# A two-layer graph attention kernel: node-id rows prepared one group ahead in the first layer, two transposes moved to the end of the step in the second

## The chip, the cores and the metric

The kernel runs on one core of a Trainium2 chip. A core has five engines with queues of their own that work in parallel and wait for each other through semaphores: PE (matmul), DVE (vector), ACT (activation), POOL (here it only issues gathers) and SP (plain transfers). The metric is the time of one execution on the device in microseconds (us); lower is better.

## The reference

The input is a graph of 3125 nodes with 128 features and 53125 edges, sorted by destination. Two attention layers run one after the other, each on the normalised node features and added to them.

```
h = relu(layernorm(x));  x = x + L0(h)     # e = leaky(a_src[src] + a_dst[dst]), 8 heads
h = relu(layernorm(x));  x = x + L1(h)     # e = q[dst] . k[src] / 4 + edge_attr @ We + be
# both: m = segment_max(e, dst); p = exp(e - m[dst]); out = segment_sum(p * v[src], dst) / segment_sum(p, dst)
```

L1 ends with an output projection and a layer norm. The edge attributes (32 per edge) are used by L1 alone, but their product with We is computed along with L0.

## The kernel before

Nodes are cut into 25 blocks of 125, edges into 416 tiles of 128. A tile and a block that meet are a "visit": 440 visits. 16 visits make a group (28 groups; the last has 8 visits), four visits a quarter. Each layer is one loop over `step(g)`, g from 0 to 29, written out in full, once for each engine. Its order on each engine is the order of the code; what ties the engines together are counting semaphores. In one step three groups are worked on:

- group g (`new`): its one-hot matrices S (edge x node in the block) are made by ACT (`one_hot`, L632 and L636, 4 visits at a time). The source rows are gathered from a table in memory into G by POOL (L528, one gather of 128 rows per visit, 16 per group). The destination side is spread to the edges by a matmul with ST, the transpose of S (`expand`, PE). DVE forms the scores.
- group g-1 (`mid`, called q): scores are transposed on PE (L874, L875; semaphore `scoreT`), scanned along the edges on DVE, and maxima are passed between visits by two small products on PE (`hop1`, L891, and `hop2`, L904). From the maxima follow differences DD (DVE), exponentials EP (ACT), their transposes on PE (L945, L946, `pT`), a factor per node (L951, `al_mm`, then ACT L682), and the softmax columns of PV (ACT L693, `pcols`).
- group g-2 (`old`, called r): DVE multiplies the gathered rows by the columns (`weigh`, L1408, four quarters), PE sums them by node (`sums`, L857, six batches of 3, 3, 2, 3, 3, 2 visits; `mm_done`), DVE adds the sums to `acc` (`add`, L1431, 16 of them).

How ST is made differs. In the second layer PE transposes S (`one_hot_T`, L828, four transposes per quarter) into one of two banks tp, and ACT copies it (`evac`, L642). In the first layer PE spreads a row of node ids over 125 partitions (`spread_ids`, L821, a matmul with ones, from `lid_ring`) into tp, and DVE compares it with the partition's own number (`node_rows`, L1220), which gives a bf16 ST_b. tp has two banks, so quarter 2 waits for the use of quarter 0. In the first layer tp[0] also takes the transposes of the edge attributes (L938, `a_T`), which ACT copies to attrT (L678, `a_Te`) for the product with We (L916).

POOL's order is plain: 16 gathers for each group, group after group, three groups deep. A function `pace` holds it back at every fourth gather by waits on PE's semaphores. In the first layer gather 0 of group g waits for `expanded` of the quarters 0 and 1 of group g-1 and for eight sums of step g-1, gather 8 for `scoreT` of step g, gather 12 for `hop1`. Those waits don't appear in the diff. In the second layer gather 8 waits for transposes and sums of the step before, and gather 0 waits for the first `weigh` of the group whose place in G it takes.

```python
                        wait(pool, s["expanded"], 4 * q + 2)
                        if r >= 0:
                            wait(pool, s["mm_done"], GV * r + 8)
```

## Time and profile before

| | us |
|---|---|
| median of 3 timed runs | 1561.53 |
| lowest, highest | 1558.28, 1563.58 |
| the profiled run | 1565.84 |
| its span, first to last instruction | 1564.1 |

In the profiled run PE is busy for 65% of the span, DVE for 60%, POOL for 56% and ACT for 41%. The first layer's loop takes roughly 60 to 730 us of the span, the second layer's 820 to 1520 us. Times in the rows further down count from the start of the span. The number in brackets at a row's end is how long the engine had stood idle before the instruction, and what ended it; "remote" and "issue" name no instruction. An operation's start on PE is its launch; its result can be seen later.

### The profile page before, as it was taken

Reading aid. Unit: us, or ns where it says so; the run is one execution under the profiler, and the core shown is the slowest. Engines: PE = TensorE matmul, PEld = TensorE weight load, DVE = VectorE, ACT = ScalarE, POOL = GpSimd, SP = SyncE. Lnnn points to the kernel's source line nnn. Section 1 sums busy time; section 2 is a strip of 40 time slices with the busy share of each in tenths; the row PEclk is TensorE's granted clock in tenths of the full one; section 3 lists DMA queues with packets and bytes.
Section 4 is the critical chain, followed back from the end, with each engine's and each line's share of the span. In section 5 each row is a group of like instructions: output and inputs, shape, how many; then the busy total and the mean of one; then the engine's idle time right before and its main releaser. Section 6 shows DMA issues by size and latency. Waiting matters only on the chain. (4 is left out here: it accounts for less than half of the span.)

```text
span 1564.1 us, 21265 instructions
## 1 busy us (share of the span) xinstructions
PE 1022.3 (65%) x4985; PEld 859.9 (55%) x4985; DVE 934.4 (60%) x3002; ACT 638.2 (41%) x1699; POOL 880.9 (56%) x926
## 2 busy tenths in 40 slices
PE   5546666656757766667475567666767767676775
PEld 4335554545545555555365456656656666565664
DVE  6446656556566655657823465656566565656577
ACT  5524343343434434422463344434344444444414
POOL 5756666666666666662056566665666555666400
PEclk9655556565565555655776687787776676778665
DMA  6322222222222222122133232322232222332201
GB/s 138 80 55 54 60 51 60 52 59 61 54 57 54 61 60 55 45 60 80 51 109 95 79 85 85 88 84 78 83 87 85 81 85 81 85 88 84 68 1 42
DMA packets 56924, 110.37 MB, mean 71 GB/s; under 512 B 17421, under 2 KB 31393, under 8 KB 56677
## 3 DMA queue, kind: packets, MB, share of 16 engines
q0 software_dynamic: 36288, 91.12, 22.5%
q1 hardware_dynamic: 19203, 17.39, 3.9%
q8 instruction: 47, 0.77, 0.2%
q10 hardware_dynamic: 1313, 0.50, 0.1%
q14 instruction: 73, 0.59, 0.1%
HBM read 100.60 MB, written 8.81 MB: 70 GB/s over the span
## 5 line engine op out<-in xcount | busy, mean ns | idle before, releaser
L528 POOL DMA_INDIRECT G<-table,idx_all x880 | 854.6, 971 | 524.2 <-issue 272.7
L857 PE MATMUL bank<-PV,S 128*125 128x144 f32 x1760 | 456.3, 420 | 134.2 <-DVE acc L1431 79.7
L857 PEld LDWEIGHTS bank<-PV,S 128*125 128x125 f32 x1760 | 379.8, 291 | 157.6 <-issue 82.5
L1431 DVE TENSOR_TENSOR acc<-acc,bank 125x144 f32 x880 | 260.3, 296 | 291.0 <-PE bank L857 155.4
L632 ACT ACTIVATE S<-iota_n,lid 128x125 f32<-128x125 f32 x880 | 275.8, 387 | 0.4 <-issue 0.4
L841 PE MATMUL bank<-qe,ST 125*128 x880 | 163.6, 355 | 93.4 <-DVE prod L1230 67.8
L841 PEld LDWEIGHTS bank<-qe,ST 125*128 125x128 f32 x880 | 152.6, 264 | 106.1 <-issue 106.1
L642 ACT ACTIVATE ST<-bank 125x512 f32<-125x512 f32 x110 | 63.7, 595 | 284.5 <-PE bank L828 153.2
L1408 DVE TENSOR_TENSOR PV<-G,PV 128x512 f32<-128x512 f32 x220 | 151.1, 688 | 22.4 <-issue 20.8
L636 ACT ACTIVATE S<-S,ones 128x500 f32<-128x500 f32 x220 | 156.6, 712 | 8.9 <-ACT S L632 1.9
L828 PE MATMUL bank<-ident,S 128*125 128x128 f32 x440 | 101.1, 369 | 30.7 <-issue 24.2
L828 PEld LDWEIGHTS bank<-ident,S 128*125 128x125 f32 x440 | 82.9, 263 | 38.5 <-issue 29.4
L1220 DVE TENSOR_SCALAR ST<-bank,vcol 125x512 bf16<-125x512 f32 x110 | 81.5, 743 | 33.2 <-remote 30.5
L1338 DVE TENSOR_TENSOR CCM<-bank,Vsel 128x32 f32<-128x32 f32 x56 | 10.7, 191 | 150.6 <-remote 116.0
L667 ACT ACTIVATE EP<-DD 128x256 f32<-128x256 f32 (+1 forms) x56 | 20.3, 363 | 189.5 <-DVE DD L1372 189.5
L1230 DVE TENSOR_TENSOR prod<-bank,G 128x512 f32<-128x512 f32 x110 | 74.6, 678 | 24.7 <-remote 19.8
L904 PE MATMUL bank<-D,HselT 8*128 8x16 f32 x224 | 51.9, 347 | 39.5 <-DVE D L1331 23.1
L904 PEld LDWEIGHTS bank<-D,HselT 8*128 8x128 f32 x224 | 46.4, 287 | 52.8 <-DVE D L1322 29.8
L1239 DVE TENSOR_REDUCE raw<-prod 128x32 f32<-128x512 f32 x110 | 74.3, 675 | 1.1
L682 ACT ACTIVATE AL<-bank 125x8 f32<-125x8 f32 x56 | 9.9, 177 | 156.3 <-PE bank L951 96.3
L875 PE MATMUL bank<-ident,sc 128*128 128x128 f32 x56 | 20.9, 373 | 69.6 <-issue 38.1
L916 PE MATMUL bank<-WeBD,attrT 128*128 128x32 f32 x208 | 49.0, 400 | 26.2 <-DVE CCM L1338 15.1
(219 smaller groups left out, 1125.7 us busy)
## 6 DMA issues: line engine op xcount, KB each, us to landing
G<-table,idx_all POOLq DMA_INDIRECT x880
prod<-in_edge_attr_dram SPq DMA_DIRECT2D x26, 224.0 KB
table<-G SPq DMA_DIRECT2D x12, 224.0 KB
bias_rows<-qe SPq DMA_DIRECT2D x1, 1664.0 KB
table<-h0b SPq DMA_DIRECT2D x8, 178.5 KB
out_dram<-G SPq DMA_DIRECT2D x8, 168.0 KB
prod<-in_edge_attr_dram SPq DMA_DIRECT2D x26, 30.0 KB
xs<-in_x_dram SPq DMA_DIRECT2D x1, 504.0 KB
```

The lines of the kernel that those rows point to most:

```text
L528: pool.indirect_dma_start(G[:, u, v, 0:w], None, table, bass.IndirectOffsetOnAxis(ap=idx_all[:, g * GV + v:g * GV + v + 1], axis=0)).then_ ...
L632: last = act.activation(S[:, u, v, :], iota_n[:, 0:BN], ACT.Abs, bias=lid[:, bass.ds(g * GV + v, 1)], scale=-1.0)
L636: act.activation(S[:, u, QV * j:QV * j + QV, :], S[:, u, QV * j:QV * j + QV, :], ACT.Relu, bias=ones[:, 0:1], scale=-1.0).then_inc(s.sem[" ...
L828: last = pe.transpose(tp[j % 2][0:BN, k * P:k * P + P], S[:, u, QV * j + k, :], ident[:, :])
L841: last = pe.matmul(ex[j % 2][:, k * F:k * F + F], ST[:, v, :], nodes[:, bass.ds(off, F)], start=True, stop=True)
L857: pe.matmul(sums_bank(p)[0:BN, at:at + H * SLOT], S[:, ur, v, :], PV[:, v, :, :].rearrange("p h k -> p (h k)"), start=True, stop=True).the ...
L904: last = pe.matmul(sm[:, 64 + GV * k:64 + GV * k + GV], HselT[:, :, :].rearrange("p v h -> p (v h)"), d[:, k, k:k + GV], start=True, stop= ...
L1220: ve.tensor_scalar(ST_b[:, QV * j:QV * j + QV, :], tp[j % 2][0:BN, :].rearrange("p (v e) -> p v e", v=QV), node, None, op0=ALU.is_equal).t ...
L1230: ve.tensor_tensor(prod[:, j % 2, :].rearrange("p (v f) -> p v f", v=QV), ex[j % 2][:, :].rearrange("p (v f) -> p v f", v=QV), G[:, u, QV ...
L1239: ve.tensor_reduce(raw[:, QV * j:QV * j + QV, :].rearrange("p v h -> p (v h)"), prod[:, j % 2, :].rearrange("p (c d) -> p c d", d=DH), AX. ...
L1408: ve.tensor_tensor(PV[:, QV * j:QV * j + QV, :, 0:DH], rows, PV[:, QV * j:QV * j + QV, :, DH:DH + 1].to_broadcast([P, QV, H, DH]), ALU.mul ...
L1431: ve.tensor_tensor(a, a, o, ALU.add).then_inc(s.sem["acc_added"], 1)
```

## The change

In the first layer all four id rows of group g+1 are spread and compared in step g, into the other half of ST_b, which now has two (`g % 2`). PE spreads quarters 0 and 1 after the third batch of sums and 2 and 3 before the fifth. DVE compares after its adds 7, 8, 11 and 13. The expansions 0 and 1 stand after the first and second batch of sums. The attribute transposes of group q are made in step q+1, right after the score transpose, and ACT copies them as its first operation of the step, ahead of esT; before, they were made in step q ahead of `pT`. In the second layer the transposes 0 and 1 of group g+1 are made at the end of step g on PE, and copied at the end of step g on ACT; the one-hots 2 and 3 come ahead of the copies 2 and 3, and PE's transposes 2 and 3 and expansions 0 and 1 change places.

```diff
-        ST_b = ST_[0:BN, :, :].rearrange("p v e -> p (v e)").bitcast(BF16)[:, 0:GV * P].rearrange("p (v e) -> p v e", v=GV)
+        ST_b = ST_[0:BN, :, :].rearrange("p v e -> p (v e)").bitcast(BF16).rearrange("p (d v e) -> p d v e", d=2, v=GV)
...
+                    if n == 0 and mid and q < AG:
+                        wait(act, a_T, q + 1)
+                        wait(act, a_mm, q)
+                        act.activation(attrT[:, :], tp[0][:, :], ACT.Copy).then_inc(a_Te, 1)
                     if mid and n == 0:
                         wait(act, s["scoreT"], q + 1)
                         wait(act, s["dd_ready"], 2 * q)
...
                         if g == 0:
                             one_hot(g, u, 0)
                             one_hot(g, u, 1)
-                        for j in range(new):
+                            evac(g, 0)
+                            evac(g, 1)
+                        for j in range(2, new):
+                            one_hot(g, u, j)
+                        for j in range(2, new):
                             evac(g, j)
-                            if j + 2 < new:
-                                one_hot(g, u, j + 2)
...
                         act.activation(eb_nat[:, bass.ds(q * (ATTR_C * H), ATTR_C * H)], sm[:, 256:256 + ATTR_C * H],
                                        ACT.Copy).then_inc(a_out, 1)
-                    if new:
-                        if n == 0 and has_attr(g, new):
-                            wait(act, a_T, g + 1)
-                            wait(act, a_mm, g)
-                            act.activation(attrT[:, :], tp[0][:, :], ACT.Copy).then_inc(a_Te, 1)
...
                         wait(act, s["mm_done"], GV * q)
                         act.activation(PV[:, :, :, DH:DH + k].rearrange("p v h k -> p (v h) k"),
                                        sT[:, 2 * P:(2 + k) * P].rearrange("p (k c) -> p c k", k=k), ACT.Copy).then_inc(s.sem["pcols"], 1)
+                    for j in range(min(quarters(g + 1), 2) if n else 0):
+                        evac(g + 1, j)
...
                     wait(pe, s["st_ready"], 4 * g + j - 1)
-                    if j == 0:
-                        wait(pe, a_Te, attr_done(g - 1))
+                    if j == 0 and g > 1:
+                        wait(pe, a_Te, attr_done(g - 2))
                     pe.matmul(tp[j % 2][0:BN, :], ones_b[32 * u:32 * u + 1, :], lid_ring[32 * u:32 * u + 1, j * QV * P:(j + 1) * QV * P],
                               start=True, stop=True).then_inc(s.sem["t_done"], 1)
...
-                        last = pe.matmul(ex[v // 8][:, v % 8 * width:(v % 8 + 1) * width], ST_b[:, v, :],
+                        last = pe.matmul(ex[v // 8][:, v % 8 * width:(v % 8 + 1) * width], ST_b[:, g % 2, v, :],
...
-                    if new and n == 0:
-                        spread_ids(g, u, i, 0)
-                        spread_ids(g, u, i, 1)
+                    ahead, ua, ia = quarters(g + 1), (g + 1) % UNROLL, (g + 1) // UNROLL
+                    if n == 0 and g == 0:
+                        for j in range(new):
+                            spread_ids(g, u, i, j)
...
                         pe.transpose(sT[:, 0:P], sc[:, :, :].rearrange("p v h -> p (v h)"), ident[:, :]).then_inc(s.sem["scoreT"], 1)
+                    if n == 0 and mid and q < AG:
+                        pe.wait_ge(s_attr[q % UNROLL], 48 * (q // UNROLL + 1))
+                        wait(pe, a_Te, q)
+                        wait(pe, s["st_ready"], 4 * g + 3)
+                        for k in range(QV):
+                            last = pe.transpose(tp[0][:, k * P:k * P + P], attr_in[:, q % UNROLL, k * P:k * P + P], ident[:, :])
+                        last.then_inc(a_T, 1)
                     if new:
                         pe.load(regs, offs[1 if n else 2][:, bass.ds(g * GV, GV)])
-                    if new and n:
+                    if n and g == 0:
                         one_hot_T(g, u, 0)
+                        one_hot_T(g, u, 1)
                     if 3 * old > 0:
                         sums(g, u, 0)
-                    for j in range(2, 0 if n else new):
-                        spread_ids(g, u, i, j)
+                    if new and n == 0:
+                        expand(g, 0)
                     if mid:
                         wait(pe, s["rh_ready"], q + 1)
                         wait(pe, s["x_done"], q)
@@ -892,8 +904,10 @@
                                   start=True, stop=True).then_inc(s.sem["hop1"], 1)
                     if 3 * old > 2:
                         sums(g, u, 1)
-                    if new and n:
-                        one_hot_T(g, u, 1)
+                    if new > 1 and n == 0:
+                        expand(g, 1)
+                    if new > 2 and n:
+                        one_hot_T(g, u, 2)
                     if mid:
                         wait(pe, s["x_done"], q + 1)
                         wait(pe, s["u_done"], q + 1)
@@ -904,11 +918,8 @@
                             last = pe.matmul(sm[:, 64 + GV * k:64 + GV * k + GV], HselT[:, :, :].rearrange("p v h -> p (v h)"),
                                              d[:, k, k:k + GV], start=True, stop=True)
                         last.then_inc(s.sem["hop2"], 1)
...
-                    if new and n == 0:
+                    if new and n:
                         expand(g, 0)
-                        expand(g, 1)
-                    if new > 2 and n:
-                        one_hot_T(g, u, 2)
                     if n == 0 and mid and q < AG:
                         wait(pe, a_Te, q + 1)
                         wait(pe, s["cc_mul"], q + 1)
@@ -918,25 +929,22 @@
                         last.then_inc(a_mm, 1)
                     if 3 * old > 4:
                         sums(g, u, 2)
-                    if new and n:
-                        expand(g, 0)
-                        expand(g, 1)
+                    for j in range(0 if n else min(ahead, 2)):
...
+                        spread_ids(g + 1, ua, ia, j)
                     if new > 3 and n:
                         one_hot_T(g, u, 3)
+                    if new and n:
+                        expand(g, 1)
                     if 3 * old > 6:
                         sums(g, u, 3)
                     if new > 2:
                         expand(g, 2)
                     if new > 3:
                         expand(g, 3)
+                    for j in range(2, 0 if n else ahead):
+                        spread_ids(g + 1, ua, ia, j)
                     if 3 * old > 8:
                         sums(g, u, 4)
-                    if n == 0 and has_attr(g, new):
-                        pe.wait_ge(s_attr[u], 48 * (i + 1))
-                        wait(pe, a_Te, g)
-                        for k in range(QV):
-                            last = pe.transpose(tp[0][:, k * P:k * P + P], attr_in[:, u, k * P:k * P + P], ident[:, :])
-                        last.then_inc(a_T, 1)
...
                     if 3 * old > 10:
                         sums(g, u, 5)
+                    for j in range(min(quarters(g + 1), 2) if n else 0):
+                        one_hot_T(g + 1, (g + 1) % UNROLL, j)
                 run_groups(step)
...
-                    def node_rows(j):
-                        if j >= new or n == 1:
-                            return
-                        wait(ve, s["t_done"], 4 * g + j + 1)
-                        wait(ve, s["expanded"], 4 * (g - 1) + j + 1)
-                        ve.tensor_scalar(ST_b[:, QV * j:QV * j + QV, :],
+                    def node_rows(to, j):
+                        if j >= quarters(to) or n == 1:
+                            return
+                        wait(ve, s["t_done"], 4 * to + j + 1)
+                        wait(ve, s["expanded"], 4 * (to - 2) + j + 1)
+                        ve.tensor_scalar(ST_b[:, to % 2, QV * j:QV * j + QV, :],
                                          tp[j % 2][0:BN, :].rearrange("p (v e) -> p v e", v=QV), node, None,
                                          op0=ALU.is_equal).then_inc(s.sem["st_ready"], 1)
...
-                    node_rows(0)
+                    if g == 0:
+                        for j in range(4):
+                            node_rows(g, j)
                     load_offsets(0)
                     weigh(0)
-                    node_rows(1)
                     load_offsets(1)
                     loop_max()
                     weigh(1)
                     edge_scans()
                     rescale()
                     edge_maxima()
-                    node_rows(2)
                     add(0)
                     visit_scans()
                     add(1)
                     carry()
-                    node_rows(3)
                     add(2)
                     weigh(2)
...
                     differences()
                     weigh(3)
                     add(7)
+                    node_rows(g + 1, 0)
                     shrink()
                     qk_product(0)
                     add(8)
+                    node_rows(g + 1, 1)
                     shrink_heads()
                     qk_sum(0)
                     add(9)
@@ -1474,10 +1485,12 @@
                     loop_weights()
                     qk_sum(1)
                     add(11)
+                    node_rows(g + 1, 2)
                     qk_product(2)
                     add(12)
                     qk_sum(2)
                     add(13)
+                    node_rows(g + 1, 3)
                     qk_product(3)
                     part_sum(1)
                     score_sum()
```

PE in the first layer, around the score transpose (L874, L875) between two steps. First before, then in the changed kernel, where these lines are L878 and L879; L951 is L959, L857 is L860, and L938 is L885.

```order
790 L951 MATMUL bank<-R,OHF 125x8
791 L857 MATMUL bank<-PV,S 125x144 x2
792 L821 MATMUL bank<-lid_ring,ones_b 125x512 x2
793 L874 MATMUL bank<-ident,es 128x128
794 L875 MATMUL bank<-ident,sc 128x128
795 L877 TENSOR_LOAD rows
796 L857 MATMUL bank<-PV,S 125x144 x3
797 L821 MATMUL bank<-lid_ring,ones_b 125x512 x2
798 L891 MATMUL bank<-RH,Hsel 8x32
```

```order
354 L959 MATMUL bank<-R,OHF 125x8
355 L860 MATMUL bank<-PV,S 125x144 x2
356 L878 MATMUL bank<-ident,es 128x128
357 L879 MATMUL bank<-ident,sc 128x128
358 L885 MATMUL bank<-ident,prod 128x128 x4
359 L888 TENSOR_LOAD rows
360 L860 MATMUL bank<-PV,S 125x144 x3
```

The two spreads L821 ahead of the score transpose are gone, and the four attribute transposes follow it.

DVE in the first layer, after the multiply of quarter 3 (L1408, now L1418). L1220, now L1230, is the compare, L1431, now L1441, an add.

```order
846 L1408 TENSOR_TENSOR PV<-G,PV 128x32x16
847 L1431 ISA
848 L1431 TENSOR_TENSOR acc<-acc,bank 125x144
849 L1383 TENSOR_SCALAR DF<-DF 8x1
850 L1431 ISA
851 L1431 TENSOR_TENSOR acc<-acc,bank 125x144
852 L1390 TENSOR_SCALAR R<-ident,DF 8x8
```

```order
844 L1418 TENSOR_TENSOR PV<-G,PV 128x32x16
845 L1441 ISA
846 L1441 TENSOR_TENSOR acc<-acc,bank 125x144
847 L1230 TENSOR_SCALAR ST<-bank,vcol 125x512
848 L1393 TENSOR_SCALAR DF<-DF 8x1
849 L1441 ISA
850 L1441 TENSOR_TENSOR acc<-acc,bank 125x144
851 L1230 TENSOR_SCALAR ST<-bank,vcol 125x512
852 L1400 TENSOR_SCALAR R<-ident,DF 8x8
```

Two of the four compares now stand after the adds 7 and 8, ahead of the scores of the same step. Before they came after the scores (L1278):

```order
867 L1278 SCALAR_TENSOR_TENSOR sc<-raw 128x128
868 L1431 ISA
869 L1431 TENSOR_TENSOR acc<-acc,bank 125x144
870 L1431 ISA
871 L1431 TENSOR_TENSOR acc<-acc,bank 125x144
872 L1260 TENSOR_TENSOR xs<-xs,rowv 125x128
873 L1220 TENSOR_SCALAR ST<-bank,vcol 125x512
874 L1211 TENSOR_LOAD rows
875 L1212 ISA
876 L1408 TENSOR_TENSOR PV<-G,PV 128x32x16
877 L1220 TENSOR_SCALAR ST<-bank,vcol 125x512
```

PE in the second layer, end of one step and start of the next; L828, now L831, are the transposes of S.

```order
1937 L951 MATMUL bank<-R,OHF 125x8
1938 L857 MATMUL bank<-PV,S 125x144 x2
1939 L875 MATMUL bank<-ident,sc 128x128
1940 L877 TENSOR_LOAD rows
1941 L828 MATMUL bank<-ident,S 125x128 x4
1942 L857 MATMUL bank<-PV,S 125x144 x3
1943 L891 MATMUL bank<-RH,Hsel 8x32
1944 L857 MATMUL bank<-PV,S 125x144 x3
1945 L828 MATMUL bank<-ident,S 125x128 x4
```

```order
2515 L959 MATMUL bank<-R,OHF 125x8
2516 L860 MATMUL bank<-PV,S 125x144 x2
2517 L831 MATMUL bank<-ident,S 125x128 x8
2518 L879 MATMUL bank<-ident,sc 128x128
2519 L888 TENSOR_LOAD rows
2520 L860 MATMUL bank<-PV,S 125x144 x3
2521 L903 MATMUL bank<-RH,Hsel 8x32
2522 L860 MATMUL bank<-PV,S 125x144 x3
2523 L831 MATMUL bank<-ident,S 125x128 x4
```

The transposes of quarters 0 and 1 now stand ahead of the score transpose, and those of quarter 2 where quarter 1 was.

## Rows read from the trace of the kernel before

**Rows 1.** Stretches view, first layer: length, busy us by engine, granted clock, DMA share.

```profile
158.65:626.64 467.99, 312.41 (x1445) 250.32 (x1445) 284.37 (x916) 184.71 (x513) 295.21 (x305) 0.57 0.24 57
```

**Rows 2.** Groups by line, 157 to 650 us: busy us, mean ns | idle before.

```profile
L528 POOL DMA_INDIRECT G<-table,idx_all x321 | 311.4, 970 | 181.2 <-issue 117.5 <-remote 29.7 <-PE bank L857 14.6
...
L1220 DVE TENSOR_SCALAR ST<-bank,vcol 125x512 bf16<-125x512 f32 x80 | 59.4, 743 | 16.9 <-remote 14.5 <-issue 0.8 <-PE bank L821 0.8
...
L821 PE MATMUL bank<-lid_ring,ones_b 1*125 1x512 bf16 x80 | 39.2, 585 | 0.0
...
L678 ACT ACTIVATE attrT<-bank 128x512 f32<-128x512 f32 x20 | 11.9, 597 | 61.7 <-issue 43.3 <-PE bank L938 18.4
```

**Rows 3.** Timeline, POOL: start, us, operation, idle before it.

```profile
406.60 0.94 POOL L528 DMA_INDIRECT G<-table,idx_all  x1 [2.29 <-remote]
...
415.33 0.95 POOL L528 DMA_INDIRECT G<-table,idx_all  x1 [0.30 <-issue]
...
418.54 1.37 POOL L528 DMA_INDIRECT G<-table,idx_all  x1 [2.26 <-issue]
...
430.98 0.94 POOL L528 DMA_INDIRECT G<-table,idx_all  x1 [2.29 <-remote]
```

**Rows 4.** Timeline, DVE, ACT and PE in the first half of the same step.

```profile
405.95 0.30 DVE L1431 TENSOR_TENSOR acc<-acc,bank 125x144 f32 x1 [5.29 <-remote]
...
407.94 1.77 PE L857 MATMUL bank<-PV,S 128*125 128x144 f32 x6 [4.12 <-DVE acc L1431]
...
409.50 1.06 PE L938 MATMUL bank<-ident,prod 128*128 128x128 f32 x4
...
412.05 0.29 DVE L1278 SCALAR_TENSOR_TENSOR sc<-raw 128x128 f32<-128x128 f32 x1
...
412.85 0.41 ACT L693 ACTIVATE PV<-bank 128x256 f32<-128x256 f32 x1 [0.65 <-PE bank L857]
...
413.99 0.42 PE L875 MATMUL bank<-ident,sc 128*128 128x128 f32 x1
...
417.83 0.28 ACT L652 ACTIVATE esT<-bank 128x128 f32<-128x128 f32 x1 [4.58 <-remote]
...
418.20 0.29 DVE L1292 TENSOR_TENSOR smax<-bank,esT 128x128 f32<-128x128 f32 x1 [2.41 <-ACT esT L652]
```

**Rows 5.** Timeline, DVE at the end of the second half.

```profile
430.33 0.31 DVE L1431 TENSOR_TENSOR acc<-acc,bank 125x144 f32 x1 [5.28 <-remote]
```

**Rows 6.** Timeline, all engines, an earlier step.

```profile
357.76 0.94 POOL L528 DMA_INDIRECT G<-table,idx_all  x1 [2.80 <-PE bank L857]
...
367.76 0.41 ACT L693 ACTIVATE PV<-bank 128x256 f32<-128x256 f32 x1 [2.53 <-remote]
...
368.51 0.42 PE L875 MATMUL bank<-ident,sc 128*128 128x128 f32 x1
...
369.87 0.98 POOL L528 DMA_INDIRECT G<-table,idx_all  x1 [2.37 <-PE bank L875]
```

**Rows 7.** Timeline, POOL: gather 8 and the next gather 0 of another step.

```profile
294.00 1.37 POOL L528 DMA_INDIRECT G<-table,idx_all  x1 [1.64 <-issue]
...
308.30 0.94 POOL L528 DMA_INDIRECT G<-table,idx_all  x1 [4.20 <-PE bank L857]
```

**Rows 8.** Timeline, POOL in the second layer, gathers 8 and 0 of two steps.

```profile
998.25 1.54 POOL L528 DMA_INDIRECT G<-table,idx_all  x1 [2.45 <-PE bank L857]
...
1010.56 0.94 POOL L528 DMA_INDIRECT G<-table,idx_all  x1 [2.04 <-DVE PV L1408]
...
1022.78 1.53 POOL L528 DMA_INDIRECT G<-table,idx_all  x1 [2.47 <-PE bank L857]
...
1034.29 0.94 POOL L528 DMA_INDIRECT G<-table,idx_all  x1 [1.25 <-DVE PV L1408]
```

**Rows 9.** Stretches view, second layer, PE: length, busy us, granted clock, DMA share.

```profile
1001.00:1005.00 4.00, 4.00 (x24) 0.68 0.36 106
1024.50:1028.50 4.00, 3.29 (x25) 1.00 0.34 98
```

## The prediction

> **What bounds the kernel now.** I read the totals of the first layer first, then the gathers in order of time, then the engines around them. In the steady part of the first layer no engine is busy all the time: PE is busy for 312 of 468 us, DVE for 284, and POOL, which only issues gathers, for 295 [rows 1]. But POOL's gathers set the beat. There are 321 of them in 493 us [rows 2], 24.6 us for the 16 of one group, which is one step of the loop. They follow each other in 1.25 us, so 16 alone need 20 us. The rest is two pauses per step. The rows show one step: eight gathers from 406.60 to 415.33, a pause, eight from 418.54, a pause, and the next group at 430.98 [rows 3]. I call the stretch from gather 0 to gather 8 of a group the first half (11.94 us) and that from gather 8 to the next gather 0 the second half (12.44 us).
>
> What ends the pauses is seen on the other engines. In the first half POOL waits for the score transpose L875. PE starts it at 413.99 for 0.42 us, so it should be done at 414.4. ACT, which copies its result (esT, L652), starts only at 417.83 after 4.58 us of idling, and DVE waits 2.41 us for that copy [rows 4]. So PE's result is noticed some 3.4 us after it should be there, and 2.5 us after the last of the eight gathers was issued. In the second half the same: DVE has waited 5.28 us when the sums of PE let it go on at 430.33, and POOL's next gather follows at 430.98 [rows 3, 5]; the same wait (5.29 us) ended at 405.95 [rows 4]. My reading: while gathers are in flight, results of PE that fall late in a batch of eight are reported late, and all are out once the batch has drained. Each half is then 8 x 1.25 us and some 2 us of drain, whatever PE or DVE do, as long as what POOL waits for is executed before the drain.
>
> The Trainium skill, "TensorE: Matmul & The Clock Gate", section "The cost: per-tile semaphore tail", puts an increment by a matmul at some 26 ns. By that the pause before gather 8 would not exist now, the first half would be 10 us, and the 3.0 us moved below would lengthen it by up to 1 us. The trace disagrees (3.4 us for one transpose), and the row decides.
>
> **First layer, first half.** Four compares of spread ids (node rows, L1220, 0.743 us each [rows 2]) leave the head of DVE's step and stand between the adds ahead of the scores. DVE's total stays, but 4 x 0.74 = 3.0 us moves into the chain from 405.95 to the scores, which start at 412.05 [rows 4]: they come at 415.3. On PE the spreads 2 and 3 (L821, 0.585 us [rows 2]) now stand ahead of the batch of sums that started at 407.94, and wait for the first two compares: 2 x 0.74 + 0.58, about 2.1 us later. Behind these sums follow two transposes, a small product and the last sums; four attr transposes (1.06 us together) no longer stand between them. So the last sums are executed 1 to 1.3 us later, and the softmax columns that started at 412.85 could start near 414. The score transpose waits for columns and scores, and its two spreads are gone from in front of it. With no trouble it ends near 416.2. POOL reaches gather 8 at 416.58 and is released at 417.8. So the 3.0 us have a cover, the drain, of which 1.5 us remain: price 0 within it.
>
> But the columns now hang on results in the late part of the batch. The nearest row is a step in which that already happens: the columns start at 367.76, 10.0 us after gather 0, the transpose at 368.51, and gather 8 follows at 369.87, a half of 12.11 us against 11.94 [rows 3, 6]. I take this row, since it is the same chain as late as the change may make it: +0.17 us. The lower bound is -0.5 us, where the transpose has fewer results queued before it and is reported ahead of the drain. The upper bound is that the columns wait for the full drain. From columns to gather 8 it is 2.11 us [rows 6], from the report of the transpose (417.8) to gather 8 it is 0.7 [rows 3, 4]: +1.4 us.
>
> **First layer, second half.** The attr transposes now follow the score transpose, and ACT copies them (L678, 0.597 us [rows 2]) before esT, which feeds the maxima, the scans and the first hop. So the scan chain starts 0.6 us later (where the attr transposes are executed under the drain) to 1.6 us later. On the other side two compares (1.5 us) leave DVE between the first hop and the second. PE, however, now has the expansion of quarter 1 ahead of the second hop and two spreads (1.1 us) behind the next sums. Net, what POOL and DVE wait for is executed 1 to 2 us later after gather 8. It has less than the 5.28 us of DVE's wait as cover [rows 5], since PE needs part of that to execute it; in one step of before where the pattern slipped the half took 14.30 us instead of 12.44 [rows 3, 7]. The bounds are 0 and +1.9 us. I take +0.1 us, because the row of the normal step is the nearer one and most of its cover is left. Expansions 0 and 1 stand earlier and free nothing, since the scores wait for compares and last quarters.
>
> **Ends.** In the last step with edges DVE has two compares less, 2 x 0.743 = -1.5 us, with few gathers left to hide it. Step 0 keeps its four compares at its head and gets the next four behind: 3.0 us on DVE while POOL fetches three groups ahead anyway, 0.
>
> **Second layer.** Transposes 0 and 1 of S for the next group (L828) move to the end of the step, ahead of the score transpose, and their copies (L642) behind the columns on ACT, which makes the one-hots 2 and 3 before any copy. The first half here ends in a drain as above. The second (gather 8 at 998.25, next gather 0 at 1010.56, 12.31 us) ends with DVE's multiply L1408 [rows 8], at the end of a chain on DVE whose order stays, and PE's work within it (expansions 2 and 3, a batch of sums) stays in place. The score transpose gets up to 1 us later, behind a one-hot that ACT has only just made, but DVE multiplies twice before it reads it. So 0, with bounds of +0.3 us per step (7 us in all) if it is seen, and of rival 3.
>
> **Sum.** 23 steps x (0.17 + 0.1) = +6.2, less 1.5: about +5 us on the profiled 1565.84 us, 1570.8. The profiled run is 4.3 us above the median of the timed ones; on the median 1561.5 + 5 = 1566.5.
>
> **Rivals.**
> 1. The columns are caught by the drain. It decides when PE's last sums of a step are executed later than about 8 us after gather 0; before, the columns started at 6.25. For: they move by over 1 us, into the late part. Against: [rows 6], 0.17 us. Up to 1.4 x 23 = +32 us, 1593; in half of the steps, 1578.
> 2. The attr copy ahead of esT pushes the second hop into the late part of the second batch, and the sums behind it miss the drain. 1.9 us in a quarter of the steps is +11 us, 1573.
> 3. Faster, by PE's clock in the second layer. The second half takes 12.31 us where the granted clock over its expansions was 0.68, and 11.51 us (1022.78 to 1034.29) where it was 1.00, 2.4 GHz [rows 8, 9]. The two moved transposes fill an idle stretch of PE. If that brings the fast clock to the expansions in 10 to 24 of 26 steps, it is -8 to -19 us, 1543 to 1554. Against: they run some 15 us ahead of them. The same page of the Trainium skill, section "What's actually happening", has activity lift the throttle; by that rule this rival would win.
> 4. Faster, since it is not the gathers but the spreads in front of the score transpose that delay its report. Then gather 8 could start up to 1.9 us earlier: up to -40 us, 1522. Against: DVE's waits of 5.28 us end without a spread in front.
> 5. Nothing to see: all of it is under the drains, and the end gives 1 us: 1560 to 1563.
>
> **Numbers.** The forecast (1562 to 1573) has 0.45, split at the border of 0.3% (4.7 us, about what a measurement of this kernel can tell from no change): 0.23 same, 0.22 slower. Rival 1 has 0.17 and rival 2 0.09, slower. Rival 3 has 0.13 and rival 4 0.06, faster. Rival 5 has 0.10, same. So faster 0.19, same 0.33, slower 0.48. The range leaves out the worst of rival 1, the best of rival 3 and rival 4: 1551 to 1586.
>
> **What would show it.** First halves near 12.1 us, with the columns 9 to 10 us after gather 0 and the score transpose (L879) started just before the drain: the forecast. Columns at 11 us or later: rival 1. Second halves of 13 us and more: rival 2. DVE should still idle about 5 us before the add that follows the node maxima. In the second layer, halves and waits as before; halves of 11.5 us in most steps mean rival 3. First halves of 10 us prove my reading of the drain wrong, and rival 4 right.

## The result, and the profile after

The changed kernel takes 1573.88 us (median; 1564.32 to 1578.26) beside 1561.53 us for the kernel before. The ratio is 1.0064, 95% interval 1.0040 to 1.0087: slower by 6 to 14 us. (The medians alone are 12.35 us apart, a little more than the ratio gives.) The forecast was 1566.5 us, and slower was its likeliest side. The profiled run took 1577.22 us with a span of 1575.5, against 1565.84 and 1564.1.

I cut both spans at the score transposes (L875 before, L879 after; each layer has 28, counted here from 0). The first layer's 23 steps between transposes 3 and 26 grew from 565.5 to 573.7 us (+8.2), those of the second shrank from 583.0 to 581.7 (-1.3). The start grew by 1.0, the stretch between the layers by 2.7 and the end by 0.8, in all +11.4. These are two single traces; further down two traces of an unchanged first layer differ by 7.0 us.

The stretches view of the changed kernel over the same 468 us as [rows 1], with the same columns, and over 600 us of the second layer:

```profile
158.65:626.64 467.99, 330.54 (x1421) 259.67 (x1419) 275.91 (x891) 180.67 (x508) 285.74 (x299) 0.53 0.23 56
850.00:1450.00 600.00, 409.70 (x2079) 368.20 (x2080) 351.85 (x1080) 248.09 (x648) 371.45 (x380) 0.74 0.29 84
```

In the first layer POOL issued 299 gathers where it had issued 305. PE made 24 matmuls fewer and was busy for 18 us more, since its granted clock fell from 0.57 to 0.53. In the second layer the clock was 0.74 in both kernels, with 409.7 and 409.9 us of PE.

POOL in a regular step (answers [rows 3]; gather 12 of one group, gather 4 of the next, gather 12), and then in a long one (gathers 4 and 15, then the next gather 0):

```profile
404.68 0.95 POOL L528 DMA_INDIRECT G<-table,idx_all  x1 [2.33 <-issue]
...
414.20 0.95 POOL L528 DMA_INDIRECT G<-table,idx_all  x1 [0.31 <-issue]
416.94 0.94 POOL L528 DMA_INDIRECT G<-table,idx_all  x1 [1.79 <-PE bank L860]
...
428.94 0.95 POOL L528 DMA_INDIRECT G<-table,idx_all  x1 [2.30 <-issue]
```

```profile
314.36 0.95 POOL L528 DMA_INDIRECT G<-table,idx_all  x1 [2.83 <-PE bank L860]
...
328.76 0.95 POOL L528 DMA_INDIRECT G<-table,idx_all  x1 [0.30 <-issue]
335.64 0.95 POOL L528 DMA_INDIRECT G<-table,idx_all  x1 [5.93 <-PE bank L860]
```

There are still two pauses a step, but at gathers 4 and 12, not 0 and 8. The regular step is as long as before, 12.26 + 12.00 us against 11.94 + 12.44. The long step has one run of twelve gathers and then 5.93 us without one.

What answers [rows 4]: PE's score transpose, ACT's two copies, DVE's maxima, the first hop, and what DVE waits for after it.

```profile
420.20 0.42 PE L879 MATMUL bank<-ident,sc 128*128 128x128 f32 x1
420.42 1.06 PE L885 MATMUL bank<-ident,prod 128*128 128x128 f32 x4
421.51 0.60 ACT L652 ACTIVATE attrT<-bank 128x512 f32<-128x512 f32 x1 [3.32 <-PE bank L885]
422.01 0.27 ACT L656 ACTIVATE esT<-bank 128x128 f32<-128x128 f32 x1
422.37 0.29 DVE L1302 TENSOR_TENSOR smax<-bank,esT 128x128 f32<-128x128 f32 x1 [0.45 <-issue]
...
424.31 0.28 PE L903 MATMUL bank<-RH,Hsel 128*8 128x32 f32 x2 [0.36 <-issue]
...
428.23 0.23 DVE L1332 TENSOR_TENSOR_SCAN D<-rows,D,bank 8x16 f32<-8x16 f32 x1 [3.74 <-remote]
```

The score transpose starts 3.3 us after a pause and is seen at once: ACT copies the attribute transposes as they end (421.48), and esT right behind. What is held now is the first hop. It should be done at 424.6, and DVE notices it at 428.23, when the last gather (issued at 425.69) is 2.5 us old.

The long step on PE and DVE. PE waits 6.14 us for DVE, and DVE 5.67 us for the second hop, executed at 325.13:

```profile
325.13 0.58 PE L918 MATMUL bank<-D,HselT 8*128 8x16 f32 x4 [1.50 <-DVE D L1334]
331.85 1.89 PE L927 MATMUL bank<-WeBD,attrT 128*128 128x32 f32 x8 [6.14 <-DVE CCM L1348]
...
331.51 0.19 DVE L1348 TENSOR_TENSOR CCM<-bank,Vsel 128x32 f32<-128x32 f32 x1 [5.67 <-remote]
```

Here the first hop was seen before POOL had to wait for it (DVE used it at 324.30, 0.7 us after a gather and with the run going on), so POOL reached gather 12 with its condition met and went on. The second hop fell into the late part of a run that was now twelve long. Three steps took 27.8, 27.7 and 27.6 us, against 24.3 to 24.5 for a regular one, and were followed by 24.7, 26.2 and 24.3. Before, long steps were mostly paid back: 27.5 + 20.9, 29.0 + 20.6, 28.8 + 21.0, 27.8 + 20.5.

The second layer (answers [rows 8]), gathers 8 and 0 of a step:

```profile
1014.15 1.54 POOL L528 DMA_INDIRECT G<-table,idx_all  x1 [2.51 <-PE bank L860]
...
1026.52 0.95 POOL L528 DMA_INDIRECT G<-table,idx_all  x1 [2.06 <-DVE PV L1418]
```

12.37 us, as the 12.31 before, and the same engines end the pauses.

### The profile page after: what moved, and what is told of

Its sections match the earlier page's. It is cut to its first block, busy times and chain, and to the rows that moved or that the text cites. A ratio compares the mean times of both kernels' runs of the same rounds, so it can differ in the third digit from the quotient of the medians.

```text
span 1575.5 us, 21262 instructions
## 1 busy us (share of the span) xinstructions
PE 1054.7 (67%) x4985; PEld 882.9 (56%) x4985; DVE 932.8 (59%) x3002; ACT 637.9 (40%) x1699; POOL 878.3 (56%) x926
## 4 chain that ended last, share of the span: by engine, by line
PE 35%; DVE 26%; issue 18%; another core or an unknown queue 15%; DVEq 4%; ACT 2%; POOL 0%; POOLq 0%; ACTq 0%
PE bank L860 15%; DVE acc L1441 6%; PE bank L844 6%; DVE PV L1418 4%; PE bank L824 3%; PE bank L927 3%; PE bank L918 3%; DVE prod L1240 2%; PE bank L831 2%; DVE ST L1230 1%; DVE raw L1249 1%; DVEq L87 1%; DVEq L1222 1%; DVE FR L1314 1%
## 5 line engine op out<-in xcount | busy, mean ns | idle before, releaser
L860 PE MATMUL bank<-PV,S 128*125 128x144 f32 x1760 | 473.3, 428 | 79.5 <-DVE PV L1418 53.2
L860 PEld LDWEIGHTS bank<-PV,S 128*125 128x125 f32 x1760 | 386.3, 295 | 133.9 <-issue 125.5
L1441 DVE TENSOR_TENSOR acc<-acc,bank 125x144 f32 x880 | 259.9, 295 | 283.5 <-PE bank L860 189.7
L844 PE MATMUL bank<-qe,ST 125*128 x880 | 178.9, 373 | 100.1 <-DVE prod L1240 95.2
L844 PEld LDWEIGHTS bank<-qe,ST 125*128 125x128 f32 x880 | 161.5, 275 | 108.6 <-issue 107.5
L1418 DVE TENSOR_TENSOR PV<-G,PV 128x512 f32<-128x512 f32 x220 | 151.4, 689 | 33.7 <-issue 33.7
L831 PE MATMUL bank<-ident,S 128*125 128x128 f32 x440 | 90.3, 341 | 40.6 <-ACT S L636 20.5
L831 PEld LDWEIGHTS bank<-ident,S 128*125 128x125 f32 x440 | 79.3, 249 | 47.2 <-issue 23.7
L1230 DVE TENSOR_SCALAR ST<-bank,vcol 125x512 bf16<-125x512 f32 x110 | 81.2, 742 | 17.8 <-remote 17.6
L824 PE MATMUL bank<-lid_ring,ones_b 1*125 1x512 bf16 x110 | 67.8, 669 | 30.2 <-DVE ST L1230 22.4
```

The lines of the kernel that those rows point to most:

```text
L824: pe.matmul(tp[j % 2][0:BN, :], ones_b[32 * u:32 * u + 1, :], lid_ring[32 * u:32 * u + 1, j * QV * P:(j + 1) * QV * P], start=True, stop=T ...
L831: last = pe.transpose(tp[j % 2][0:BN, k * P:k * P + P], S[:, u, QV * j + k, :], ident[:, :])
L844: last = pe.matmul(ex[j % 2][:, k * F:k * F + F], ST[:, v, :], nodes[:, bass.ds(off, F)], start=True, stop=True)
L860: pe.matmul(sums_bank(p)[0:BN, at:at + H * SLOT], S[:, ur, v, :], PV[:, v, :, :].rearrange("p h k -> p (h k)"), start=True, stop=True).the ...
L1230: ve.tensor_scalar(ST_b[:, to % 2, QV * j:QV * j + QV, :], tp[j % 2][0:BN, :].rearrange("p (v e) -> p v e", v=QV), node, None, op0=ALU.is_ ...
L1418: ve.tensor_tensor(PV[:, QV * j:QV * j + QV, :, 0:DH], rows, PV[:, QV * j:QV * j + QV, :, DH:DH + 1].to_broadcast([P, QV, H, DH]), ALU.mul ...
```

## The experiments

The comparisons ran on several chips and fell into two kinds. In one the kernel before took 1561 to 1597 us, in the other 1325. I call them the **held** and the **prompt** kind, for what the traces show below. No chip is known to have been used for two comparisons, so "prompt chip" below means the chip of a prompt comparison: whether the kind belongs to the chip or to something else about the place and hour of the run was not tested. Only the kernel before was timed on both kinds.

### The two halves of the change, prompt kind

**first_only** is the changed kernel with the second layer's order as before.

> The first layer's part of the change alone; the second layer is as before. In the trace of the changed kernel the 23 steps from 3 to 26 of the first layer take 573.7 us against 565.5 before (+8.2), those of the second layer 581.7 against 583.0. If the loss is the first layer's, this kernel is +7 to +12 us on before (ratio 1.004 to 1.008) and within 3 us of the changed kernel. If the second layer takes part in it by its ends (the longer stretch between the layers, the last steps), it is +4 us or less.

**second_only** is the kernel before with the second layer's order of the change.

> The second layer's part of the change alone. My reading: nothing is to be seen, -2 to +2 us on before (ratio 0.999 to 1.001), and the second halves of the steps with the low clock stay near 12.3 us. Rival (the clock of TensorE over the expansions): more steps at 11.5 us, -8 us or more. Other rival (the second layer costs the few us that the first does not explain): +3 us or more.

The kernel before took 1325.07 us here. first_only took 1318.23, ratio 0.9951 (0.9928 to 0.9973): faster. second_only took 1345.99, ratio 1.0163 (1.0125 to 1.0201): slower. first_only was faster where I had it slower, and second_only slower where my reading had nothing. The first thing to read is the first layer itself, first_only's gathers and adds from 157 to 620 us:

```profile
L528 POOL DMA_INDIRECT G<-table,idx_all x349 | 348.3, 998 | 106.4 <-issue 97.8 <-PE bank L856 7.6 <-DVE PV L1412 0.9
L1435 DVE TENSOR_TENSOR acc<-acc,bank 125x144 f32 x358 | 105.5, 295 | 65.4 <-PE bank L856 55.7 <-issue 0.8
```

POOL fits 349 gathers into 463 us, one in 1.33 us, where it had one in 1.54 [rows 2]. No pause over 2 us is left, and no idling in this stretch is put down to remote. PE's results are seen while gathers fly; PE, ACT and POOL of first_only:

```profile
415.64 1.06 PE L881 MATMUL bank<-ident,prod 128*128 128x128 f32 x4
...
416.74 0.60 ACT L652 ACTIVATE attrT<-bank 128x512 f32<-128x512 f32 x1 [2.65 <-PE bank L881]
...
415.37 0.94 POOL L528 DMA_INDIRECT G<-table,idx_all  x1 [0.30 <-issue]
416.62 1.33 POOL L528 DMA_INDIRECT G<-table,idx_all  x1 [0.30 <-issue]
```

ACT starts 0.04 us after the transposes end. In the steps 3 to 26, the first layer takes 21.1 us a step in second_only (its order there is the old one) and 20.9 in first_only, near the 20.0 that 16 gathers of 1.25 us need. Under the old order DVE's sum of L1275 waits for the last gathers of its group:

```profile
L1275 DVE TENSOR_TENSOR raw<-es,G 128x128 f32<-128x128 f32 x28 | 8.2, 292 | 109.8 <-DMA G<-table,idx_all 109.8
```

That is 3.9 us a step over the whole layer. From 157 to 620 us it is 3.6 us a step, and 0.7 in first_only. So on prompt chips the gathers come near to setting the first layer, without any drain, and its new order gives 0.2 us a step.

The second layer there, by score transposes 3 to 26: 474.3 us in first_only, 489.5 in second_only. The stretches view of 860 to 1240 us, first_only and then second_only (columns as above):

```profile
860.00:1240.00 380.00, 262.58 (x1692) 231.37 (x1693) 283.29 (x875) 197.47 (x521) 289.96 (x296) 0.84 0.36 103
```

```profile
860.00:1240.00 380.00, 294.63 (x1607) 262.89 (x1607) 272.97 (x840) 188.03 (x499) 289.25 (x295) 0.76 0.36 103
```

POOL issues the same number of gathers, but PE does 5% fewer matmuls and is busy 12% longer, at a clock of 0.76 against 0.84. The engines fall behind POOL step by step: the score transpose comes 24 us after its gather 0 at the layer's start in both, at its end 24 in first_only and 40 in second_only. The debt is paid after the last gather, 82.5 us against 65.0. Groups by line show two new idle times of PE in second_only, 860 to 1100 us:

```profile
L861 PE MATMUL bank<-PV,S 128*125 128x144 f32 x363 | 80.9, 371 | 19.7 <-DVE PV L1414 19.7
...
L845 PE MATMUL bank<-qe,ST 125*128 x368 | 65.1, 332 | 14.0 <-DVE prod L1236 14.0
...
L832 PE MATMUL bank<-ident,S 128*125 128x128 f32 x180 | 36.6, 339 | 13.6 <-ACT S L636 13.6
```

and for first_only, the same work:

```profile
L856 PE MATMUL bank<-PV,S 128*125 128x144 f32 x378 | 75.6, 343 | 0.0
...
L840 PE MATMUL bank<-qe,ST 125*128 x384 | 51.1, 281 | 12.7 <-DVE prod L1234 12.7
...
L827 PE MATMUL bank<-ident,S 128*125 128x128 f32 x188 | 36.7, 326 | 8.7 <-issue 8.7
```

Transpose 2 waits some 1.2 us a step for the one-hot that ACT makes late, and the sums wait for `weigh`. One expansion matmul takes 332 ns, not 281.

### Two variants of the changed kernel, prompt kind

```diff
+                    if mid and n == 0:
...
                     if n == 0 and mid and q < AG:
...
-                    if mid and n == 0:
...
```

**est_first** exchanges these two copies on ACT: esT is copied ahead of attrT.

> The changed kernel with one edit: ACT copies esT, which feeds the maxima, ahead of attrT in the first layer. Rival (the copy of the attributes ahead of esT pushes the second hop late, and the late sums make the long steps): the loss goes, -8 us on the changed kernel, near 1562. My reading (the long steps come from a first hop that is reported before POOL has reached gather 12, so that POOL issues twelve gathers on end): nothing, or a few us more, since the first hop comes earlier still: 0 to +5 us on the changed kernel, 1573 to 1579.

```diff
-                            wait(pool, s["mm_done"], GV * r + 19)
+                            wait(pool, s["mm_done"], GV * r + 20)
```

**pace20** lets gather 12 wait for one more sum.

> The changed kernel with one number changed: in the first layer POOL's gather 12 waits for one more sum (mm_done 16r+20 instead of 16r+19, the first of the sums that follow the first hop on PE). My reading: three steps of the changed kernel (at 188, 315 and 539 us) have no pause at gather 12, a batch of 12 gathers of 14.4 us, and take 27.6 us instead of 24.4. With the later wait the pause at gather 12 is there in every step, these three steps take 24.4 us, and 7 to 9 us are won: 1565 to 1567, near before. Rival (the long steps are something else, and less freedom for POOL costs time): no change or slower than 1574.

est_first took 1338.79 us (1.0102, 1.0066 to 1.0139) and pace20 1341.82 (1.0116, 1.0078 to 1.0154). Both have the 82 us behind the last gather. The halves, -0.5% and +1.6%, add up to about these. The changed kernel itself was not timed on this kind. In the first layer est_first takes 20.7 us a step and pace20 20.9. There are no runs of twelve with a pause on this kind, so pace20 could not test its theory.

### The same questions where results are held

**before_again** is the kernel before, for its trace.

> The kernel before itself, for its trace beside the others of these comparisons. In the first four of them the kernel before took 1325 us, not 1561, and steps of 20.6 to 21.1 us, with no pauses of 2.3 us at all, stand in all traces. My reading: whether results of PE are held while gathers are in flight is a property of the place of the run and not of the kernel. Then this trace has, beside a median near 1325, no pause over 2 us, DVE's idling of 5.3 us before the add is gone, and the steps of the first layer are some 21.1 us, those of the second 20.6, with 65 us behind the last gather. Beside a median near 1560 it has pauses as in the first trace.

**after_again** is the changed kernel.

> The changed kernel beside the others. If the two halves of the change add up where nothing is held (first layer -0.5%, second +1.6%), it is 1.010 to 1.012 of before, some +14 us, with 82 us behind its last gather instead of 65. Where results are held it is 1.004 to 1.009, as in the first comparison.

**first_est** is first_only with the exchange of est_first.

> The first layer's part of the change alone, with esT copied ahead of attrT on ACT. Where nothing is held: the first layer with esT first took 20.69 us a step against 20.90 with attrT first and 21.09 before, so 23 steps make -4 to -5 us on the first layer's part alone: ratio 0.990 to 0.993, 1312 to 1316 us. If the order of the two copies has no part in it: 0.995. Where results are held: +0 to +8 us on before.

**end_only** is second_only without its exchanges on PE:

```diff
-                    if new > 2 and n:
-                        one_hot_T(g, u, 2)
                     if mid:
                         wait(pe, s["x_done"], q + 1)
...
-                    if new and n:
-                        expand(g, 0)
+                    if new > 2 and n:
+                        one_hot_T(g, u, 2)
...
-                    if new > 3 and n:
-                        one_hot_T(g, u, 3)
                     if new and n:
+                        expand(g, 0)
                         expand(g, 1)
+                    if new > 3 and n:
+                        one_hot_T(g, u, 3)
```

> The second layer's part without its exchange on PE: transposes 0 and 1 of the next group stand at the end of the step and their copies too, but transpose 2 stays behind the second hop and the expansions 0 and 1 stay together behind the third batch of sums. Theory A (transpose 2 waits some 1.2 us a step for the one-hot that ACT makes late, and the second hop is queued behind it): the steps of the second layer are near 20.6 us again, ratio 0.998 to 1.003. Theory B (the copies 0 and 1 and the transposes at the end of the step are what costs, by the later score transpose and the lower clock): steps of 21.4 us and 1.012 to 1.018, as with the exchange. Where results are held neither shows.

The kernel before took 1591.13 us. after_again took 1608.55 us, ratio 1.0122 (1.0071 to 1.0172); first_est 1603.77, 1.0096 (1.0062 to 1.0130); end_only 1592.35, 1.0006 (0.9967 to 1.0046). Both kernels with the new first layer lost more than I had expected (up to 1.009, and up to 8 us). So in this held comparison the loss is in the first layer's part, and for the moves at the end of the second layer's step none is seen, to within 0.5%. esT ahead of attrT doesn't remove it. Whether end_only differs from second_only could not be seen here.

The four traces of this comparison agree with that, but single traces scatter. Between transposes 3 and 26 the first layer took 585.0 us in after_again and 585.6 in first_est, against 571.7 in before_again and 578.7 in end_only, which have the same first layer. The traced run of before_again (1600.86 us) was 10 us above the median of before, that of after_again (1601.67) the fastest of its six: as a whole they are equally long, and only their parts can be set side by side.

The trace of after_again shows a cost that the first one has less of. POOL's gather 4 waits 4.3 to 4.6 us in eight of these 23 steps, and 3.6 in one; elsewhere it is 2.9 at most. (What is quoted on late_spreads below puts all nine at 4.4.) No run of twelve with a long pause behind it stands in this stretch. One of the eight:

```profile
288.11 0.94 POOL L528 DMA_INDIRECT G<-table,idx_all  x1 [0.30 <-issue]
293.41 0.94 POOL L528 DMA_INDIRECT G<-table,idx_all  x1 [4.36 <-PE bank L860]
...
289.19 0.30 DVE L1441 TENSOR_TENSOR acc<-acc,bank 125x144 f32 x1 [2.73 <-remote]
289.42 0.74 DVE L1230 TENSOR_SCALAR ST<-bank,vcol 125x512 bf16<-125x512 f32 x1
...
290.21 0.68 PE L824 MATMUL bank<-lid_ring,ones_b 1*125 1x512 bf16 x1 [2.92 <-DVE ST L1230]
290.83 1.80 PE L860 MATMUL bank<-PV,S 128*125 128x144 f32 x6
```

The chain reads: DVE's add waits 2.73 us for sums that are held; the second compare (L1230) sits behind it; PE's spread 3 waits 2.92 us for that compare; and the fifth batch of sums, on which gather 4 waits, is queued behind the spread. So a held result now reaches PE and delays the very batch that POOL wants. Note when the add goes on: 1.1 us after the last gather was issued (288.11), not 2.5.

### Is it the gathers that hold the results?

**few_gathers** leaves out three of four gathers in the first layer:

```diff
+                            if n == 0 and g >= UNROLL and v % QV:
+                                continue
```

(The counts in the waits for gathers are changed to match.)

> The kernel before, but in the first layer from the fourth group on POOL makes only one gather of the four of a quarter (the other rows of G keep what was in them, so the first layer's sums are of old rows); everything else is as before. It asks whether the gathers in flight are what holds PE's results back. Where results are held (before near 1560 to 1600): if the gathers do it, POOL has only 5 us of gathers in a step, the pauses lose their cause, the copy of the transposed scores starts within 1 us of the transpose, and a step falls from 24.6 to what the engines need, 17 to 21 us: 85 to 170 us less. If something else holds them, the steps stay at 24 us and DVE still idles 5 us. Where nothing is held (before near 1325): the steps of 21.1 us fall to 17 to 20 if the gathers set them (25 to 90 us less), and stay if the chain of DVE and PE sets them.

**before_nopace** takes POOL's waits on PE away in the first layer:

```diff
-                if v % 4:
+                if v % 4 or n == 0:
                     return
```

> The kernel before without POOL's waits on PE at every fourth gather of the first layer; POOL is then held back only where G has no free place. Where results are held: by my reading the results wait for gathers in flight to land, so longer runs of gathers hold them longer; nothing is won, 24.6 us a step or more, POOL's pauses are fewer and longer. Rival (a pause is only gather time lost): 20.0 us a step, some 100 us less. Where nothing is held: the waits cost 1.1 us of the step's 21.1; without them 20.0 to 20.6, 10 to 25 us less, or nothing if DVE and PE set the step.

The kernel before took 1597.0 us, the held kind. few_gathers took 1407.23 us, ratio 0.8818 (0.8681 to 0.8955), a step 17.5 us, some 190 us less and more than the 85 to 170 that I had written. Its second layer keeps all its gathers, and there, in the same execution, a step still takes 25.5 us and results are still held: DVE's line L1340 alone idles 68.7 us with "remote" behind it from 860 to 1240 us. So it is the gathers that hold the results. PE, ACT and POOL of the first layer, where before ACT had waited 4.58 us for esT [rows 4]:

```profile
310.63 0.27 PE L877 MATMUL bank<-ident,sc 128*128 128x128 f32 x1
...
310.94 0.28 ACT L654 ACTIVATE esT<-bank 128x128 f32<-128x128 f32 x1 [0.61 <-PE bank L877]
...
311.65 0.94 POOL L530 DMA_INDIRECT G<-table,idx_all  x1 [1.83 <-PE bank L877]
```

The copy starts 0.04 us after the transpose ends. (The Trainium skill, "TensorE: Matmul & The Clock Gate", section "The cost: per-tile semaphore tail", gives some 26 ns for each increment of a semaphore. The 40 ns of this row are of that order, while in [rows 4] the same report took 3.4 us.) From 157 to 470 us nothing is put down to remote here.

before_nopace took 1644.57 us, ratio 1.0305 (1.0152 to 1.0459), a step 26.5 us. Its POOL makes twelve gathers, a pause, four, a pause, and DVE pays:

```profile
386.97 0.95 POOL L528 DMA_INDIRECT G<-table,idx_all  x1 [2.84 <-DVE PV L1408]
...
400.97 0.94 POOL L528 DMA_INDIRECT G<-table,idx_all  x1 [0.30 <-issue]
406.25 0.94 POOL L528 DMA_INDIRECT G<-table,idx_all  x1 [4.34 <-DVE PV L1408]
...
404.42 0.30 DVE L1431 TENSOR_TENSOR acc<-acc,bank 125x144 f32 x1 [7.67 <-remote]
```

The add waits 7.67 us and goes on 3.5 us after the twelfth gather was issued; in most other steps of this trace it waits 9.9 to 10.3 us and goes on after 3.3 to 3.7. The longer run held the sums longer, as expected, and this resembles the changed kernel's long steps. The rival, that a pause is only gather time lost, is out by some 150 us.

### Taking the two suspects away

**late_spreads** moves two spreads behind the fifth batch:

```diff
-                    for j in range(2, 0 if n else ahead):
-                        spread_ids(g + 1, ua, ia, j)
                     if 3 * old > 8:
                         sums(g, u, 4)
+                    for j in range(2, 0 if n else ahead):
+                        spread_ids(g + 1, ua, ia, j)
```

> The changed kernel with two instructions of PE moved: in the first layer the spreads 2 and 3 of the next group stand behind the fifth batch of sums, not ahead of it. In the trace of the changed kernel beside a before of 1591 us, POOL's gather 4 waits 4.4 us and not 2.5 in nine of the steps 3 to 26; each time the second of these spreads waits for DVE's second compare, which sits behind an add whose sums are reported only when the gathers have landed, and the fifth batch of sums, on which gather 4 waits, is queued behind the spread. My theory: with the spreads behind the batch the pauses of over 4 us at gather 4 are gone (2.0 to 2.3 us beyond the cadence), worth 9 to 15 us where they occurred: 0.997 to 1.003 of before. Rival (the later scores, 3 us of compares ahead of them, are what costs; the spread's wait is only where it shows): the pauses only move, to gather 12 or to the next gather 4, and the kernel stays at 1.006 to 1.012. Where results are not held (before near 1325), this edit shows nothing in the first layer, and the kernel is at 1.010 to 1.016 by its second layer, with 82 us behind its last gather.

Beside a before of 1566.86 us it took 1581.03, ratio 1.0067 (1.0031 to 1.0103). The wait that it was to remove is gone. The spreads from 157 to 650 us, after_again, then late_spreads:

```profile
L824 PE MATMUL bank<-lid_ring,ones_b 1*125 1x512 bf16 x80 | 49.5, 669 | 33.1 <-DVE ST L1230 30.3 <-DVE acc L1441 2.2 <-issue 0.7
```

```profile
L824 PE MATMUL bank<-lid_ring,ones_b 1*125 1x512 bf16 x80 | 43.5, 629 | 4.9 <-issue 3.3 <-DVE ST L1230 1.5
```

No wait over 3 us is left at gather 4. But two others came, of 6.03 us before a gather 0 and 5.21 us before a gather 12, each behind a run of twelve, and the ratio is that of the changed kernel in the first comparison (1.0064), whose trace had only 6.7 us of this wait. So the edit's gain was not shown, and the ratio fell where the rival, that slips only move, had put it (1.006 to 1.012), not where my theory had (0.997 to 1.003). The traced run, 1571.18 us, was one of the faster ones, 10 us below its kernel's median, so the trace shows little of the loss. The edit was never timed beside the changed kernel, nor where there was more of this wait to win.

**late_pace** has both edits, late_spreads and pace20.

> The changed kernel with both edits: spreads 2 and 3 behind the fifth batch of sums, and gather 12 waiting for one more sum (mm_done 16r+20). With the spreads moved alone, the pauses over 4 us at gather 4 were gone, but the kernel stayed at 1.0067 of a before of 1567 us; what is left in its trace are steps in which POOL makes twelve gathers on end (at 310, 505 and 545 us), two of them with a pause of over 6 us behind. Theory: these runs of twelve are the rest of the loss. Where results are held, a wait for a sum behind the first hop splits them: no run of twelve whose hop came early, steps of 24.4 to 24.6 us, 1 to 8 us less than before or equal to it, 0.995 to 1.002. Rival (any slip of the pattern costs about the same, and this wait only moves it): runs of twelve or pauses over 4 us still stand at other places, 1.004 to 1.012. Where results are not held: 1.010 to 1.016 by the second layer, as the changed kernel with this wait alone.

It ran beside a before of 1325.35 us, the prompt kind: 1341.83 us, 1.0115 (1.0078 to 1.0152), 20.9 us a step in the first layer and 82.4 us behind the last gather, as the changed kernel's relatives. The theory on runs of twelve was therefore not tested by taking them away. It rests on the first trace and on before_nopace, and after_again lost as much or more without them.

## Why the prediction was right, and where its steps were not

**The sum: +5 us.** Side and range were right, the size was not: 6 to 14 us by the interval, 12.35 between the medians. 1573.88 us lies just above the 1562 to 1573 that I called the forecast, and it is luck that rival 2 had been priced at 1573. The stretch between the layers grew by 2.7 in the traces where I had -1.5, and step 0 was put at nothing (the start grew by 1.0).

**The drain reading** was right in the main. few_gathers and before_nopace show from both sides that gathers in flight hold PE's results. Two things it did not have. It holds for one of the two kinds of comparison only. And "all are out once the batch has drained" is not so in every row: many held results are seen 2.4 to 3.1 us after a run's last gather was issued, but others sooner: the add in after_again's row went on after 1.1 us, and the first hop of the long step 0.7 us after a gather, with the run going on. Where the traces record a landing (first_only and second_only), no gather landed in under 2.5 us (median 2.7). So which gathers a result waits for is open.

**First layer, first half: 0.17 us a step, "price 0 within the cover".** The total was near, the place was wrong. The columns start 7.7 to 9.8 us after gather 0, mostly at 7.8, not at 9 to 10, and the score transpose is not "just before the drain" but 9.3 to 11.6 us after its gather 0, mostly at 10.4, in the early part of a new run, where it is reported at once. Gather 8 has lost its pause, and gathers 4 and 12 have one. I had costed a shift of 3 us inside a fixed pattern of runs; the pattern itself shifted by half a run. The regular step stayed at 24.4 us, so this did no harm to the sum.

**First layer, second half: 0.1 us a step from bounds of 0 and 1.9.** Probably too small. Together with the first half I had 6.2 us for 23 steps; the first pair of traces has 8.2, and the traces of the held comparison 6.3 to 13.9, depending on which two are set side by side, and two traces of the same layer lie 7.0 us apart. What was missing in the working is the wait that the change adds: the prediction counted the two spreads as 1.1 us of PE "behind the next sums", and did not ask what they wait for. They wait for compares that sit behind a held add, with the fifth batch queued behind them. This is what the trace of after_again shows; that it makes the loss was not shown, since late_spreads, without the wait, stayed at 1.0067. The other missing item is the run of twelve, when the first hop is seen early; only the first trace has its long steps. The step of 14.30 us [rows 7] had been the hint that a slip costs 2 us; I gave it too little.

**PE's clock in the first layer** was no term at all. It fell from 0.57 to 0.53. Whether that helped to make things late was not separated.

**The end of the layer: -1.5 us.** Not seen; what lengthened the stretch around it by 2.7 us was not looked into.

**Second layer: 0.** Right for the held kind: 581.7 us against 583.0, 590.0 against 595.9 in the second pair of traces, and end_only, with part of the order, at 1.0006. But the reason "PE's work stays in place" does not carry over: on prompt chips the same order costs 15 us in 23 steps.

**Rivals.** Rival 1 (columns caught by the drain) and rival 4 did not come. Rival 2 is out in its own form: with esT first the loss is still 0.96%. Its mechanism, a result pushed into the late part of a run so that sums miss the drain, is what the long steps of the first trace show; by my reading with another cause, the first hop seen early. Rival 3 (a faster PE clock) did not come; on prompt chips the clock went the other way, from 0.84 to 0.76. The Trainium skill, "TensorE: Matmul & The Clock Gate", section "What's actually happening", says that activity releases the throttle, and by that the filled idle stretch would have lifted the clock; the 0.74 in both held traces and the fall on prompt chips don't bear it out for this change. What took it down there is not known: PE's idle time was cut into more pieces, but no run changed that alone.

**Open:** what makes a slip be paid back in one kernel and not in the other; whether late_spreads with pace20 brings the changed kernel level on held chips; and which move of the second layer costs on prompt ones. No changed version was timed on both kinds. On the prompt kind first_only is faster than before and than all the other versions run there, but its near relative first_est is 1% slower than before on the held kind.

## What to carry to other kernels

When you move work ahead of a wait, ask of each moved instruction what it waits for in its turn, and who is queued behind it: in one trace here two cheap spreads carried a late report from DVE into the batch that paces the gathers. In a kernel whose stalls come from a held report, a shift of a few us need not stretch a half; here it changed which results fell early or late in a run, so count runs and pauses before and after. And the order of the second layer, which cost nothing that could be seen under the stall, cost 1.6% where the stall was absent, so a result from one chip is worth repeating on another.

## What was not expected of the hardware

The same program took 1325 us in two comparisons and 1561 to 1597 us in four, each on another chip as far as is recorded. The gathers' cadence is 1.25 us on both. The difference is the report of PE's results while indirect gathers are in flight: on the held kind a result that fell late in a run was seen late (the second hop of the first trace's long step 5.8 us after it should have ended), often 2.4 to 3.1 us after the run's last gather was issued, and behind runs of twelve DVE idled up to 10.3 us; on the other ACT started 0.04 us after the matmul ended. On the held kind a step with a quarter of the gathers takes 17.5 us, where the first trace of before has 24.6, so the gathers and the hold set the step, not the arithmetic. Why the two kinds differ in this is open.
